# Adding gathered expert rows onto x inside the DMA, in the last stage of an AdaLN, mixture-of-experts and mixing kernel

## The reference

```python
# layer 0: grouped convolution plus context, then top-2 of 8 experts
h = conv1d(x, L0_cond_weight, groups=4) + (cond @ c_weight.T)[:, :, None] + fside
logits = h @ W_gate + b_gate
top_idx = top_k(logits, 2)
y_all = relu(h @ W_e[e] + b_e[e])            # for each expert e
x = x + mean over the two chosen experts of y_all
# layer 1: per-sample mix of channels by softmax attention, then a 4-bit weight matrix
agg_w, agg_b = from attention over 8 kernels  # one 32x32 mix per sample
z = agg_w @ x + agg_b[:, :, None]
x = x + z @ (scales * q - zeros) + bias
```

## Time and profile before

| | |
|---|---|
| median of 3 runs | 560.36 us (559.75 to 563.19) |
| the profiled execution | 560.41 us |
| its span in the trace | 558.6 us |
| stage 3, first mix product to the end | 429.0 to 558.6 us |
| PE, DVE, ACT, POOL busy, share of the whole span | 95%, 60%, 21%, 26% |

### The profile page before, as it was taken

How to read it: one execution, slowest core, us unless ns; L and a number is a source line. 1 busy time by engine, 2 the same in 40 slices (tenths; PEclk the granted TensorE clock), 3 DMA queues, 4 the chain that set the end, 5 groups by cost and what they waited for, 6 DMA issues and landing times. The chain is left out here.

```text
span 558.6 us, 10633 instructions
## 1 busy us (share of the span) xinstructions
PE 528.9 (95%) x2614; PEld 358.9 (64%) x2615; DVE 334.5 (60%) x971; ACT 119.6 (21%) x245; POOL 143.0 (26%) x159
## 2 busy tenths in 40 slices
PE   6979999999997999999999999999978799999996
PEld 6969999999985444444444444444436577677774
DVE  3456777777764473333333333334662699999996
ACT  2212222223320111111111111111131122222221
POOL 8042444444446000000000000000005555555520
PEclk9999999999997999999999999999989899999999
DMA  4999768866524864444444444444475788888852
GB/s 114 403 304 339 226 228 268 268 213 229 199 113 150 215 191 154 151 153 154 155 153 150 151 150 150 150 152 155 141 244 162 226 271 289 267 285 295 283 190 95
DMA packets 84823, 114.33 MB, mean 205 GB/s; under 512 B 15197, under 2 KB 51853, under 8 KB 83509
## 3 DMA queue, kind: packets, MB, share of 16 engines
q1 hardware_dynamic: 57936, 56.49, 32.8%
q0 software_dynamic: 10528, 33.75, 17.7%
q10 hardware_dynamic: 16328, 23.72, 12.1%
HBM read 67.48 MB, written 46.45 MB: 204 GB/s over the span
## 5 line engine op out<-in xcount | busy, mean ns | idle before, releaser
L979 PE MATMUL bank<-we,hT 128*128 x536 | 231.0, 593 | 2.6 <-DVE hT L802 2.6
L979 PEld LDWEIGHTS bank<-we,hT 128*128 128x128 f32 x536 | 101.4, 190 | 131.0 <-issue 130.9
L448 POOL DMA_INDIRECT we<-result_d,gidx x64 | 64.9, 1014 | 293.6 <-issue 288.4
L811 DVE TENSOR_TENSOR ring_a<-bank,be_bc 128x512 f32<-128x512 f32 x71 | 48.9, 689 | 126.4 <-PE bank L979 117.2
L947 PE MATMUL bank<-wconv,phases 128*128 128x128 f32 x768 | 93.0, 279 | 3.6 <-ACT phases L472 3.6
L947 PEld LDWEIGHTS bank<-wconv,phases 128*128 128x128 f32 x768 | 90.1, 195 | 4.1 <-ACT phases L472 4.1
L523 ACT ACTIVATE ring_b<-ring_a 128x512 f32<-128x512 f32 x71 | 44.7, 630 | 207.1 <-DVE ring_a L811 199.2
L429 POOL DMA_INDIRECT lists_d<-htok,row_i x64 | 62.9, 983 | 98.1 <-issue 80.4
L802 DVE STREAM_TRANSPOSE hT<-htok 128x512 f32<-128x512 f32 x71 | 49.7, 701 | 7.7 <-DMA htok<-lists_d 7.7
L682 DVE TENSOR_TENSOR hT<-bank,rows_r 128x512 f32<-128x512 f32 x32 | 22.1, 692 | 34.4 <-PE bank L947 22.2
L1019 PE MATMUL bank<-mix_bd,we 128*128 128x128 f32 x256 | 36.7, 287 | 6.3 <-DVE we L855 2.7
(11 more groups left out here) (165 smaller groups left out, 432.3 us busy)
## 6 DMA issues: line engine op xcount, KB each, us to landing
htok<-lists_d SPq DMA_DIRECT2D x284, 64.0 KB, 2.4
result_d<-ring_b ACTq DMA_DIRECT2D x71, 256.0 KB, 2.5
xt<-in_x SPq DMA_DIRECT2D x64, 256.0 KB
we<-in_L_ffn_W_e SPq DMA_DIRECT2D x8, 1024.0 KB
out<-orow SPq DMA_DIRECT2D x32, 256.0 KB
lists_d<-orow SPq DMA_DIRECT2D x8, 256.0 KB
be_bc<-in_L_ffn_b_e ACTq DMA_DIRECT2D x1, 2048.0 KB
rows_r<-ctx_d SPq DMA_DIRECT2D x1, 1920.0 KB, 10.4
```

The source lines that it names most:

```text
L448: pool.indirect_dma_start(found[:, j, k, :], None, result_d, bass.IndirectOffsetOnAxis(ap=gidx[:, j, k:k + 1], axis=0), bounds_check=NT * ...
L811: dve.tensor_tensor(ring_a[:, j % 2, :], ps_exp[j % 2][:, :], be_bc[:, bass.ds(expert, 1), :].rearrange("p a n -> p (a n)"), ALU.add).then ...
L979: mm = pe.matmul(ps_exp[j % 2][:, :], hT[:, j % 2, p * P:(p + 1) * P], we[:, bass.ds(expert, 1), p, :].rearrange("m a n -> m (a n)"), star ...
```

## The change

Both indirect DMAs of a group now carry `compute_op=ALU.add` and write onto the x tile itself, so that the memory side of the DMA does both additions. `found`, `gidx`, the index copy on ACT and both adds on DVE go away. `y_t` becomes eight buffers (`YR = 8`) over `we[:, 0:2]`. SP loads x straight into `y_t`, up to eight groups ahead, as soon as the expert products are over (`exp_done` at 71) and for later groups as soon as `orow` of the group eight before is done. POOL issues the first gather of group g + 2, once its x is in, and then the second gather of group g, once its first has landed. Row sums come from an ACT pass over the finished y (`ACT.Copy` with `accum_out`), whose full-size output goes to a scratch tile nobody reads. PE waits for `both_in` before the mix and for `ysum_ready` before the terms. The scratch tile and `y_t` lie in memory of `we`.

```diff
@@ sync
+            sp.wait_ge(exp_done, NT)
+
             def row_step(g, j):
-                a = g + 6
+                a = g + YR
                 if live(a, NG):
-                    ja = (j + 6) % U
-                    wait(sp, ya_ready, a - 3)
-                    sp.dma_start(xt[:, ja, :], x_g[a]).then_inc(x3_in[ja], 16)
+                    wait(sp, out_ready, a - YR + 1)
+                    sp.dma_start(y_t[:, a % YR, :], x_g[a]).then_inc(x3_in[a % YR], 16)
@@ gpsimd
-            def gather(g, j):
-                wait(pool, gidx_ready, g + 1)
-                wait(pool, y_ready, g - 3)
-                pool.sem_inc(gather_go, 1)
-                for k in range(2):
-                    pool.indirect_dma_start(found[:, j, k, :], None, result_d,
-                                            bass.IndirectOffsetOnAxis(ap=gidx[:, j, k:k + 1], axis=0),
-                                            bounds_check=NT * P - 1, oob_is_err=False).then_inc(gathered[j], 16)
+            pool.wait_ge(place_ready, 1)
+            def gather(g, k):
+                pool.indirect_dma_start(y_t[:, g % YR, :], None, result_d,
+                                        bass.IndirectOffsetOnAxis(ap=place_i[:, g, k:k + 1], axis=0),
+                                        bounds_check=NT * P - 1, oob_is_err=True,
+                                        compute_op=ALU.add).then_inc((first_in, both_in)[k][g % YR], 16)
             def step3(g, j):
-                if live(g + 4, NG):
-                    gather(g + 4, (j + 4) % U)
-            unrolled(step3, -4, NG)
+                if live(g + 2, NG):
+                    pool.wait_ge(x3_in[(g + 2) % YR], (g + 2) // YR * 16 + 16)
+                    gather(g + 2, 0)
+                if live(g, NG):
+                    pool.wait_ge(first_in[g % YR], g // YR * 16 + 16)
+                    gather(g, 1)
+            unrolled(step3, -2, NG)
@@ scalar
-                a = g + 6
-                if live(a, NG):
-                    ja = (j + 6) % U
-                    wait(act, gathered[ja], (a - ja) * (32 // U))
-                    act.copy(gidx[:, ja, :], place_i[:, a, :]).then_inc(gidx_ready, 1)
+                a = g + 2
+                if live(a, NG):
+                    wait(act, both_in[a % YR], a // YR * 16 + 16)
+                    wait(act, terms_done, a - 1)
+                    act.activation(unread[:, j % 2, :], y_t[:, a % YR, :], ACT.Copy, accum_out=ysum[:, j % 2:j % 2 + 1]).then_inc(ysum_ready, 1)
@@ vector
-                    dve.tensor_tensor(y_t[:, ja, :], xt[:, ja, :], found[:, ja, 0, :], ALU.add).then_inc(ya_ready, 1)
...
-                    dve.scalar_tensor_tensor(y_t[:, ja, :], y_t[:, ja, :], 1.0, found[:, ja, 1, :], ALU.mult, ALU.add,
-                                             accum_out=ysum[:, ja % 2:ja % 2 + 1]).then_inc(y_ready, 1)
@@ tensor
-                    wait(pe, y_ready, a + 1)
+                    wait(pe, both_in[a % YR], a // YR * 16 + 16)
...
+                    wait(pe, ysum_ready, a + 1)
                     wait(pe, tlow_ready, a - 1)
```

More of the change, by code:

```diff
@@ L32 @@
 XR = 4
+YR = 8
 RS = B + 2
@@ L149, in build_program @@
         place_i = sb("place_i", [P, NG, 2], I32)
-        gidx = sb("gidx", [P, U, 2], I32)
         cond_sb = sb("cond_sb", [N, P])
@@ L183, in build_program @@
         nib_shift = sb("nib_shift", [P, 1], I32)
-        y_t = we[:, 0, :, :]
-        found = we[:, 2:4, :, :].rearrange("p e q n -> p (e q) n").rearrange("p (g k) n -> p g k n", k=2)
+        y_t = we[:, 0:2, :, :].rearrange("p e q n -> p (e q) n")
+        unread = we[:, 2, 0:2, :]
         high = sb("high", [P, 2, L], F32R)
@@ L275, in build_program @@
         result_out = [sem(f"result_out{i}") for i in range(U)]
[L276 to L281, removed]
+        x3_in = [sem(f"x3_in{i}") for i in range(YR)]
+        first_in = [sem(f"first_in{i}") for i in range(YR)]
+        both_in = [sem(f"both_in{i}") for i in range(YR)]
+        ysum_ready = sem("ysum_ready")
         mixed_done = sem("mixed_done")
@@ L383, in row_step @@
                     sp.dma_start(out_g[g], orow[:, j % 2, :]).then_inc(out_out[j % 2], 16)
-            unrolled(row_step, -6, NG)
+            unrolled(row_step, -YR, NG)
             for s in out_out:
@@ L552, in step3 @@
                     act.copy(high[:, ja, :], ps_mix[ja][:, :]).then_inc(high_ready, 1)
-                a = g + 6
+                a = g + 2
                 if live(a, NG):
-                    ja = (j + 6) % U
-                    wait(act, gathered[ja], (a - ja) * (32 // U))
-                    act.copy(gidx[:, ja, :], place_i[:, a, :]).then_inc(gidx_ready, 1)
-            act.wait_ge(place_ready, 1)
-            unrolled(step3, -6, NG)
+                    wait(act, both_in[a % YR], a // YR * 16 + 16)
+                    wait(act, terms_done, a - 1)
+                    act.activation(unread[:, j % 2, :], y_t[:, a % YR, :], ACT.Copy, accum_out=ysum[:, j % 2:j % 2 + 1]).then_inc(ysum_ready, 1)
+            unrolled(step3, -2, NG)
         @block.vector
@@ L823, in step3 @@
             def step3(g, j):
-                a, b, c, d = g + 2, g + 1, g - 1, g - 2
-                ja, jb, jd = (j + 2) % U, (j + 1) % U, (j - 2) % U
+                b, c, d = g + 1, g - 1, g - 2
+                jb, jd = (j + 1) % U, (j - 2) % U
                 if live(d, NG):
@@ L829, in step3 @@
                     wait(dve, out_out[jd % 2], (d - jd % 2) * 8)
-                    dve.tensor_tensor(orow[:, jd % 2, :], ps_lin[jd][:, :], y_t[:, jd, :], ALU.add).then_inc(out_ready, 1)
+                    dve.tensor_tensor(orow[:, jd % 2, :], ps_lin[jd][:, :], y_t[:, d % YR, :], ALU.add).then_inc(out_ready, 1)
                 if live(c, NG):
@@ L835, in step3 @@
                     dve.tensor_tensor(scaled, scaled, scale_bc[:, :], ALU.mult).then_inc(scaled_ready, 1)
-                if live(a, NG):
-                    wait(dve, x3_in[ja], ring_count(a, ja, XR))
-                    wait(dve, gathered[ja], (a - ja) * (32 // U) + 32)
-                    wait(dve, out_ready, a - 3)
-                    dve.tensor_tensor(y_t[:, ja, :], xt[:, ja, :], found[:, ja, 0, :], ALU.add).then_inc(ya_ready, 1)
                 if live(g, NG):
@@ L851, in step3 @@
                     dve.tensor_tensor(low[:, jb % 2, :], ps_mix[jb % 2][:, :], high[:, jb % 2, :].bitcast(F32), ALU.subtract).then_inc(low_ready, 1)
-                if live(a, NG):
-                    wait(dve, ya_ready, a + 1)
-                    wait(dve, terms_done, a - 1)
-                    dve.scalar_tensor_tensor(y_t[:, ja, :], y_t[:, ja, :], 1.0, found[:, ja, 1, :], ALU.mult, ALU.add,
-                                             accum_out=ysum[:, ja % 2:ja % 2 + 1]).then_inc(y_ready, 1)
-            unrolled(step3, -2, NG + 2)
+            unrolled(step3, -1, NG + 2)
         @block.tensor
@@ L1015, in step3 @@
                     ja = (j + 1) % U
-                    wait(pe, y_ready, a + 1)
+                    wait(pe, both_in[a % YR], a // YR * 16 + 16)
                     wait(pe, low_ready, a - 1)
                     for q in range(4):
-                        mm = pe.matmul(ps_mix[ja % 2][:, q * P:(q + 1) * P], y_t[:, ja, q * P:(q + 1) * P],
+                        mm = pe.matmul(ps_mix[ja % 2][:, q * P:(q + 1) * P], y_t[:, a % YR, q * P:(q + 1) * P],
                                        mix_bd[:, a, :], start=True, stop=True)
```

## The result

The changed kernel takes 606.66 us (median of 4 runs, 602.36 to 612.33); the kernel before, in the same comparison, 561.17 us. The ratio is 1.079, with a 95% interval of 1.073 to 1.085: slower by 7.9%, outside the predicted range of 550 to 590. The sign (given a chance of 0.49) and the first mechanism of the forecast were right; the size was about four times the 1.9% forecast. The ratio is taken from the three fast executions, and the profiled one is the fourth, which counts as slow (612.33 us, span 610.6, over 1.5% above the fastest), so its numbers are a few us above the median.

A forecast was written before the change was run, and what follows sets the result against it. PE sets the pace now, with DVE late; after the change the DMA engines would. Data from 424.5 us plus 181 passes at 0.74 (133.9), 11.1 for the tail and 1.8 gave 571 us, range 550 to 590.

The forecast's parts named there:

- The sign: Whole kernel: slower by over 1%, given a chance of 0.49; faster had 0.29 and same 0.22.
- the first mechanism of the forecast: Stage 3: DMA engines become the bound because adding gathers read twice; likeliest time 571 us, chance 0.46.
- What bounds the kernel: Stage 3 before the change: PE is the floor at 3.53 us a group; late DVE adds 0.18 us.
- DVE and ACT: Stage 3: DVE falls from 3.46 to about 2.0 us a group; ACT takes 1.5 to 1.6, hidden under PE.
- The gather that adds: Stage 3 DMA: each adding gather counts as two passes; 181 passes at 0.74 us make 133.9 us.
- the latency loop: Rival, waits from orow through x load and gathers: 18.8 us against 21.2 over six groups; no change, chance 0.12.
- a loaded loop: Latency loop with adding gathers landing after twice 2.7 us, x in 2.7: 22.3 us, 3.71 a group, time 561.7.
- The rival's price: POOL's issue of an adding gather: 1.0 to 2.0 us, deciding from 1.47; at 2.0, 585.2 us; chance 0.10.
- The start: Start of stage 3: x loads delay the gathers by 1 us; first mix at 431.1 against 429.0, 2.1 us lost.

The follow-up runs named there:

- e11: Changed kernel without the adds, 16 y buffers, and first gathers waiting for orow of seven groups before: 559.02 us, ratio 1.001 to the kernel before.
- e7: Changed kernel with 10 y buffers in place of 8, both adds kept: 575.22 us, ratio 1.025 to the kernel before.
- e1: Changed kernel with the add taken out of both gathers, eight y buffers kept: 569.83 us, ratio 1.022 to the kernel before.
- e9: Kernel before without the index copy on ACT, four pairs of gather buffers as before, both adds on DVE: 558.11 us, ratio 0.998.
- e6: Changed kernel with no add in the gathers and 16 y buffers: 582.3 us, ratio 1.036 to the kernel before.
- e5: Kernel before without the index copy on ACT and with eight pairs of gather buffers in place of four: 573.99 us, ratio 1.019.
- e2: Changed kernel with 16 y buffers in place of 8, both adds kept: 579.51 us, ratio 1.040 to the kernel before.

## Why the prediction was wrong in size

**What bounds the kernel.** Right. PE's own step is 3.53 us by the forecast, and 3.51 by e11, where nothing holds it. (The DMA share of 86% called "seen" is in no row; the earlier trace rows has 0.80 and 0.89. Nothing rests on it.)

**DVE and ACT.** DVE's 43% busy of 5.2 us is 2.3 us a group, near the 2.0 forecast. The ACT pass costs 632 ns and its accumulator read 189, where the bound was 83; it stays hidden, and PE's waits for it are 0.7 us in all over 450 to 590 us.

**The gather that adds.** Right in mechanism and close in size. It costs two passes, and a pass of full engines is 0.745 us of busy time in e7, where the forecast took 0.74 from the busiest window. The Trainium skill, "Collectives: The Full Stack", section "The bandwidth ceiling: the fold count and why AG ≠ RS ≠ AR", has a ratio of 1.93 between a ring collective that copies and one that adds. The trace agrees, with a measured 2.06 (1.69 against 0.82). The trace has no row for the read itself; that the second pass is the read of y is the page's account, not something a run here separated. Where the loop doesn't bind, in e7, the ratio is 1.025, and the forecast of 571 over 560.4 is 1.019. That they lie so close is in part luck: packets overlap, so by the clock a pass takes 0.262 / 381 GB/s = 0.69 us and 181 of them 9 us less than forecast, while the first mix comes 5.4 us later in e7 than forecast (436.5 for 431.1) and the engines are not full before 450 us.

**The step that failed: the latency loop.** The prediction put it as "POOL's second gather of group a stands behind the first gather of a + 2, whose x waits for `orow` of a - 6. Around that loop, six groups long", with three PE steps in it, and found 2.4 us of slack. It left out the order on PE. In a step PE does the mix of g + 1 first and the bias product of g - 1 last. So the bias product of an older group stands behind a mix that waits for data: `orow` of a - 4 can't come before the second gather of a - 2 has landed, though it needs nothing of it. The tight loop is x(a), first(a), second(a - 2), mix(a - 2), bias(a - 4), `orow`(a - 4), x(a + 4): one PE step in place of three, but only four groups. With the plain landings that the forecast used it would be 2.5 (x) + 0.8 (POOL wakes) + 1.3 (first issue) + 3.7 (second gather) + 3.8 (PE, from mix to bias product) + 0.7 (`orow`) = 12.8 us, 3.2 a group, and hidden. Loaded, it is 15.9 us even without the add (e1: x 3.9, gather 5.3), 3.97 a group; and 21.3 with it. Of the 8.5 us above 12.8, the x load has 4.0, the adding gather 1.8, its issue 0.6 and PE at its lower clock 2.1 (5.9 from mix to bias product for 3.8). So the second step that failed is the landing time: 2.5 us for an x load that took 6.5. The forecast did price a loaded loop once, but its own terms, 2.7 for x, 2.3, twice 2.7 and 11.3, add up to 21.7 us and not 22.3, which is 3.62 a group and not 3.71. The case was held to be "no change" at 0.12; it is worth 1.079 - 1.025 = 5.4%, some 30 us, by e7.

**POOL.** The rival's price was 1.0 to 2.0 us an issue, deciding from 1.47; measured 1.57. It would set 3.74 us a group if nothing else did. The other bounds ask for more (3.99 us in e7), so it does not bind, but 1.0 was the wrong end to sum with.

**The start.** Forecast 431.1 for the first mix, measured 438.6. Of the 7.5 us, 3.4 are the first gather (426.9 for 423.4: the x loads delay the stores by 4.4 us, not 1), 1.7 are three issues of 0.57 more, and 2.1 the landing of the second gather (5.85 us from its issue, not 3.7), with 0.3 for small gaps between issues. The price was taken as an average of bandwidth; what it came to is a delay in front of a single wait, the one for the last result store.

**In sum.** From before to after by the ratios: 1.001 for everything but the add, with an unbound loop and paced issues (e11, whose relief of DVE and later start cancel); 1.025 with the adds (e7, so 2.4% or 13 us for them; the two differ in buffers and pacing too, and e7 waits for its output stores); 1.079 with eight buffers. No run clearly beat the kernel before: the nearest is e9 at 0.998, whose interval includes 1.

## What to carry to other kernels

An add inside a gather moves work from an engine with some time left to DMA engines with less: look up how full they are before, and count a tile twice. When a ring feeds several engines, write the loop down with each engine's order in it, not only with who needs what; a queue that does the newest item first shortens the loop by the items it holds back, and two buffers were worth 5% here. Price the loop with landing times measured under load, the output buffers' loop too: when x loads no longer held e7 up, its output stores did.

## What the runs showed that was not expected

A long unbroken run of indirect DMA issues on POOL goes with pauses of ACT and DVE of up to 10 us: in e6 and e5, with 16 and 8 buffers of gathers ahead, both slower by 1.9 to 3.6%, and both cured by a bound on how far POOL may run ahead (e11, e9). Adding gathers, issued every 1.88 us in place of 1.32, show no such long pause in e7, nor in e2 with sixteen buffers. What holds ACT and DVE is open. The DMA share in e6 is 0.76 from 450 to 500 us, and 0.67 from 462 to 467, within the pause, so full engines are not it. In e6 no packet of the instruction queues is recorded from 424 to 473 us, and ACT is free again at 476; in e5 the next one comes at 461, after ACT is free at 459. So a late fetch is neither shown nor excluded, and no run tells it from a late semaphore.

The DMA share can read 1.08 or 1.09 when the engines are full, so 0.9 in the changed kernel left more room than its tenth.
